# Four mixtures of experts between two attentions: the fourth mixture in tiles of 384 and 256 rows, and three moves in the schedule of the others

## The chip, the core and the metric

One core of one Trainium2 chip. The time is device microseconds of one launch, the median of the runs shown; the profile is one more execution. PE is TensorE, PEld its weight loads, DVE VectorE, ACT ScalarE, POOL GpSimd, SP the queue from which most transfers are issued.

## The reference

4096 tokens of 128 numbers (8 batches of 512), all float32, go through six sublayers, each on a layernorm of x and added to x:

```python
x = x + 0.5 * L0_ffn(layernorm(x))    # mixture 1: 8 experts, top 2, no capacity
x = x + L0_attn(layernorm(x))         # softmax attention, 16 heads, rope
x = x + 0.5 * L0_ffn(layernorm(x))    # mixture 2: same weights
x = x + 0.5 * L1_ffn(layernorm(x))    # mixture 3: 16 experts, top 2, capacity 640
x = x + L1_attn(layernorm(x))         # linear attention
x = x + 0.5 * L1_ffn(layernorm(x))    # mixture 4: weights of mixture 3
# an expert: gelu(rows @ W1 + b1) @ W2 + b2, with W1 128x512 and W2 512x128
# a token whose place among its expert's rows is 640 or more is left out there
```

## The kernel before

Each mixture scatters the normalised rows by expert into a buffer in HBM, reads them back as tiles of 128 rows of one expert, runs the expert, scatters the outputs by token, reads them back by batch and combines them into X. The mixtures are f = 0 to 3 in the code, the sublayers L = 0 to 5 (f = 1 is L 2, f = 2 is L 3, the linear attention is L 4, f = 3 is L 5). There are 71 tiles in f = 0 and 1, and 79 in f = 2 and 3.

A tile takes from PE one transpose (`tile_turn`, L1479), four matmuls of 128 columns into four PSUM banks (`tile_hidden`, L1502) and four more for the output (`tile_outputs`, L1511). ACT makes four gelus (L1091). DVE copies the turned rows (`rows_turned`, L2261), makes the scatter's indices (L2272) and adds the bias (`outputs_out`, L2275). SP loads the tile's 64.5 KB of rows (L642) and its expert's 256 KB of W1 (L645) at addresses read from a table; W2 and the biases of all 16 experts stay in SBUF. POOL scatters the outputs (L846). PE, ACT and DVE look the expert's place up in the table for each tile.

Every engine has its own list of work in a fixed order. The tile loops count steps c: in step c PE turns tile c+2, does `hidden(c)` and then `outputs(c-1)`, and the routing and combining of batches are put into chosen steps. In f = 1, batch b (0 to 7) begins at step `start_of(L, b)`: two gathers (L1985), layernorm moments (L1975) and a root on DVE, scaling on ACT, turning and router logits (L1559) on PE, top two on DVE, ranks (L1413 to L1418) on PE, and slots on DVE (`place`, L2050 to L2060) at `place_of`. POOL then sends the batch's rows to the next mixture in 8 indirect transfers (`send`, L825). The eight starts are 26, 32, 41, 50, 59, 68, 74, 79, and `place_of` is 10 later. The sends of batches 0 to 4 are mixed into f = 1 one for each output scatter, each batch's from the tile after its place.

The tables of tiles are made in two parts. When the first five batches (`KNOWN1`) are counted (`count_first`, L1425), `first_table` (`first_sums`, `first_rows`: a chain of dependent DVE operations, L2160 to L2176) lists the first 25 tiles, which can start before the other batches are routed; `main_counts`, `main_sums` and `main_rows` list the rest. In f = 1 the first sums and rows for f = 2 fall into steps 70 and 71, ahead of the output of tile 70 in DVE's order. The linear attention makes the first table for f = 3 in its iteration 5, while its `logits(5)` waits for it.

f = 2 combines batches 0 to 3 between its tiles (`FRONTS` = 4, at `front_of(b)` = 50, 55, 60, 65), and the linear attention, in iterations 2 to 5, batches 4 to 7. For each of these POOL takes a deviation more there (`deviation_of`, L881 to L885) and ACT two passes instead of one. f = 3 combines six batches between its tiles (`LAST_FRONTS` = 6) and two behind them.

## Time and profile before

| | |
|---|---|
| median of 3 runs | 1451.51 us (1450.81 to 1454.0) |
| the profiled execution, its own time | 1452.39 us |
| its span, first to last instruction | 1450.5 us |
| busy: PE, PEld, DVE, ACT, POOL | 1215.6, 856.8, 916.6, 802.0, 694.4 us |
| mean granted clock of PE | 0.934 |
| moved by DMA | 229.15 MB, mean 158 GB/s |

The stages follow one another: the second mixture's tile loop ends near 903 us, the third's runs to about 1129, the linear attention to 1262, and the fourth mixture to the end. A float32 matmul shows as two records in PE's rows, a transpose as one. "x8" in a row of the timeline is eight such records in a line, and its length is that from the first's start to the last's end.

### The profile page before, as it was taken

To read this page: it belongs to the slowest core of one execution; us is meant where nothing else is said; L and a number is where in the kernel's file an instruction comes from. 1 tells how busy PE (TensorE), PEld (TensorE's weight loads), DVE (VectorE), ACT (ScalarE), POOL (GpSimd) and SP (SyncE) were. 2 spreads that over 40 slices of the span, in tenths; PEclk is the share of its full clock that TensorE was granted. 3 is DMA by queue.
4 is the path that set the end of the run, shared out by engine and by line. 5 is a ranking of instruction groups with operands and counts; after the bars stand their busy time and mean duration, and the time that the engine had idled before them with its cause. 6 is when DMAs were issued, how large, how long until landed. Compare 5 with 4: busy or idle time off the path is not lost.

```text
span 1450.5 us, 34189 instructions
## 1 busy us (share of the span) xinstructions
PE 1215.6 (84%) x8356; PEld 856.8 (59%) x8356; DVE 916.6 (63%) x3275; ACT 802.0 (55%) x2085; POOL 694.4 (48%) x931
## 2 busy tenths in 40 slices
PE   4399897999999998998689897389989766589995
PEld 3399884222323223222589786388978655489995
DVE  7534667889889999886425656363355586543344
ACT  4255542676776776767345554254555564355552
POOL 4776452222253553545644576276434276544443
PEclk9999998899999999999799999599999986599998
DMA  9787767443534524441478684466756021367785
GB/s 292 175 227 209 211 184 223 137 127 114 165 118 127 144 77 132 125 131 36 125 206 255 199 234 122 110 177 183 204 166 183 8 66 38 102 171 197 212 232 173
DMA packets 194060, 229.15 MB, mean 158 GB/s; under 512 B 28304, under 2 KB 129296, under 8 KB 193872
## 3 DMA queue, kind: packets, MB, share of 16 engines
q1 hardware_dynamic: 170704, 187.74, 47.7%
q0 software_dynamic: 17792, 36.60, 7.3%
q10 hardware_dynamic: 5376, 2.63, 0.6%
q8 instruction: 78, 1.28, 0.4%
q14 instruction: 110, 0.90, 0.2%
HBM read 156.85 MB, written 69.76 MB: 156 GB/s over the span
## 4 chain that ended last, share of the span: by engine, by line
PE 55%; DVE 22%; issue 6%; POOL 5%; ACT 5%; DMA 3%; DVEq 2%; SPq 1%; ACTq 0%; POOLq 0%
PE PS L1502 16%; PE PS L1511 15%; DVE arena L2470 6%; PE PS L1693 5%; PE PS L1669 5%; PE PS L1479 3%; POOL dispatched L825 3%; DVE X L1985 2%; ACT arena L1212 2%; PE PS L1677 2%; PE PS L1655 2%; DVE BST L1975 2%; DVEq L2269 1%; DVE arena L2261 1%; DVE arena L2275 1%
## 5 line engine op out<-in xcount | busy, mean ns | idle before, releaser
L1091 ACT ACTIVATE arena<-PS,arena 128x128 f32<-128x128 f32 x1200 | 347.4, 368 | 316.4 <-PE PS L1502 305.6
L846 POOL DMA_INDIRECT expert_out<-arena x300 | 290.8, 969 | 331.3 <-DVE arena L2272 141.3
L1212 ACT ACTIVATE arena<-PS 128x512 f32<-128x512 f32 x512 | 283.8, 596 | 135.4 <-PE PS L1669 134.4
L1502 PE MATMUL PS<-arena 128*128 128x128 f32 x2400 | 343.7, 288 | 8.9 <-ACT arena L1091 7.4
L1511 PE MATMUL PS<-arena 128*128 x2400 | 329.4, 281 | 17.8 <-DVE arena L2275 16.1
L2470 DVE TENSOR_REDUCE arena<-PS 128x2 f32<-128x1024 f32 x256 | 301.0, 1217 | 28.3 <-PE PS L1679 27.4
L1511 PEld LDWEIGHTS PS<-arena 128*128 128x128 f32 x2400 | 299.3, 196 | 24.9 <-issue 22.8
L1502 PEld LDWEIGHTS PS<-arena 128*128 128x128 f32 x2400 | 303.5, 198 | 13.7 <-issue 11.3
L2275 DVE TENSOR_TENSOR arena<-PS,arena 128x128 f32<-128x128 f32 x300 | 87.6, 292 | 232.9 <-PE PS L1511 230.6
L825 POOL DMA_INDIRECT dispatched<-arena x192 | 185.4, 966 | 89.7 <-issue 54.4
L1669 PE MATMUL PS<-arena 96*128 96x512 bf16 x512 | 174.3, 392 | 10.5 <-ACT arena L1212 5.4
L1669 PEld LDWEIGHTS PS<-arena 96*128 96x128 bf16 x512 | 45.0, 98 | 184.2 <-ACT arena L1212 148.7
L1479 PE MATMUL PS<-CST,arena 128*128 128x128 f32 x300 | 90.6, 302 | 73.1 <-DMA arena<-dispatched 36.4
L1693 PE MATMUL PS<-arena 128*18 128x512 f32 x1024 | 136.1, 605 | 1.4 <-ACT arena L1212 0.5
L2272 DVE TENSOR_TENSOR arena<-arena,CST 128x1 uint32<-128x1 f32 x300 | 48.0, 160 | 111.7 <-issue 77.7
L1013 POOL DMA_INDIRECT dispatched<-arena x64 | 62.5, 976 | 108.2 <-DVE arena L2470 92.7
L2261 DVE COPY arena<-PS 128x128 f32<-128x128 f32 x300 | 85.3, 284 | 39.8 <-PE PS L1479 21.8
L1677 PE MATMUL PS<-arena 64*128 64x512 bf16 x256 | 86.2, 398 | 19.5 <-DVE arena L2470 15.0
L1479 PEld LDWEIGHTS PS<-CST,arena 128*128 128x128 f32 x300 | 43.7, 146 | 98.2 <-issue 54.4
L1679 PE MATMUL PS<-arena 64*128 64x512 bf16 x256 | 86.2, 398 | 0.0
L1985 DVE SCALAR_TENSOR_TENSOR X<-YC,GATE,X 128x128 f32<-128x128 f32 x256 | 74.6, 353 | 6.4 <-DMA YC<-expert_out 6.2
L1677 PEld LDWEIGHTS PS<-arena 64*128 64x128 bf16 x256 | 19.0, 94 | 85.8 <-DVE arena L2470 44.4
(264 smaller groups left out, 1196.5 us busy)
## 6 DMA issues: line engine op xcount, KB each, us to landing
arena<-experts SPq DMA_DIRECT2D x300, 256.0 KB
arena<-dispatched SPq DMA_DIRECT2D x300, 64.5 KB
qk_products<-arena SPq DMA_DIRECT2D x48, 384.0 KB, 4.4
arena<-qk_products SPq DMA_DIRECT2D x64, 288.0 KB
YC<-expert_out SPq DMA_DIRECT2D x64, 256.0 KB
dispatched<-FILL SPq DMA_DIRECT2D x32, 322.5 KB, 6.5
arena<-experts SPq DMA_DIRECT2D x32, 322.0 KB, 5.8
arena<-qk_products SPq DMA_DIRECT2D x64, 128.0 KB, 5.2
```

The lines of the kernel that those rows point to most:

```text
L825: pool.indirect_dma_start(buffer_of(L), bass.IndirectOffsetOnAxis(ap=SLOT[:, k, t:t + 1], axis=0), XR[:, k, t, :], None).then_inc(s_first ...
L846: pool.indirect_dma_start(YK, bass.IndirectOffsetOnAxis(ap=ID[:, n:n + 1], axis=0), YS[:, n, :], None).then_inc(s_yo[sign_of(f, tau)], 16)
L1091: act.activation(bent(f, tau)[:, q, :], bank(q, 0, P), func, bias=arena[:, bass.ds(stay + (DOWN + q), 1)]).then_inc(s_g, 1)
L1212: act.activation(PT[:, G % 2, j, k, :], bank(4 + k % 2), ACT.Exp, scale=float(1.0 / np.sqrt(HD))).then_inc(s_exp, 1)
L1479: pe.transpose(bank(4, 0, P), XP[:, g % XRING, 0:D], ident).then_inc(s_xpt, 1)
L1502: pe.matmul(bank(q, 0, P), ups(f, tau)[:, q * P:q * P + P], turned(f, tau), start=True, stop=True).then_inc(s_h, 1)
L1511: mm = pe.matmul(bank(6, 0, P), bent(f, tau)[:, q, :], arena[:, bass.ds(stays[f, tau] + q * D, D)], start=(q == 0), stop=(q == FC - 1))
L1669: pe.matmul(bank(4 + k % 2), KS[0:STACK, G % QK_RING, j, P * k:P * k + P], QS[0:STACK, G % QK_RING, j, :], start=True, stop=True).then_inc ...
L1677: pe.matmul(bank(2 * w), QS[0:HALF, r, head, P * a:P * a + P], KS[0:HALF, r, head, :], start=True, stop=True)
L1693: mm = pe.matmul(bank(6)[32 * j:32 * j + VCOLS, :], VA[:, G // 4 % V_RING * GT + k, q % 2, j, (HD + 1) * o:(HD + 1) * o + VCOLS], PT[:, G ...
L1985: ins = dve.scalar_tensor_tensor(out=X[:, t, :], in0=YC[:, b % 2, k, j, :], scalar=GATE[:, k, t:t + 1], in1=X[:, t, :], op0=ALU.mult, op1= ...
L2470: dve.tensor_reduce(MX[:, G % 2, head:4:2, a], PS[:, 1024 * w:1024 * w + 1024].rearrange("p (a b) -> p a b", a=2), AX_X, ALU.max).then_inc ...
```

## The change

1. The fourth mixture gets functions of its own (`last_sixteen`, `tall_turn`, `tall_hidden`, `tall_gelus`, `tall_outputs`, `tall_rows`, `tall_out`, `late_table`, `tall_moe`). It has 32 tiles: one of the first 384 rows of each expert, and then one of the other 256 rows of each, in the order in which the experts passed 384 rows. A tile loads its whole expert (1156 columns of float32, 592 KB) into a ring of 4 and needs no lookup; the first 16 need no table either. Every matmul of `tall_hidden` has 384 or 256 columns. It starts when all rows have been sent. Nothing of the first table is left in it.
2. The linear attention no longer counts the first five batches nor makes the first table, and `logits(5)` waits for nothing of it.
3. f = 1: the eight starts become 24, 29, 38, 47, 56, 65, 73, 79, and `place_of` is 7 later instead of 10. The outputs of a batch are loaded at `start + 4` in SP's order instead of `start + 2`. `last_step` becomes 90 instead of 93.
4. f = 2: `FRONTS` = 6, at `front_of(b)` = 47, 52, 57, 62, 67, 72, so batches 4 and 5 leave the linear attention. In f = 3 four batches are combined between tiles, and four behind them. ACT issues the loads of the first four.

```diff
-MOE = [dict(E=E0, S=S0, tiles=TOKENS * 2 // (S0 * P) + E0 - 1), dict(E=E1, S=S0, tiles=TOKENS * 2 // (S0 * P) + E1 - 1)]
+MAIN, SHORT = 3, S1 - 3
+MOE = [dict(E=E0, S=S0, tiles=TOKENS * 2 // (S0 * P) + E0 - 1), dict(E=E1, S=S0, tiles=TOKENS * 2 // (S0 * P) + E1 - 1),
+       dict(E=E1, S=MAIN, tiles=2 * E1)]
...
-FRONTS, LAST_FRONTS = 4, 6
+RING = 4
+FRONTS, LAST_FRONTS = 6, 4
...
+        def late_to(b):
+            return E1 + min(E1, (b + 1) * GT * P * 2 // (MAIN * P + 1))
+        def late_front(b):
+            return late_to(b) + 6
...
-            return max(wide_to(b) + 10, 50 + 5 * b)
+            return max(wide_to(b) + 7, 47 + 5 * b)
...
             if carries(L):
                 if b >= NG - 2:
-                    return MOE[0]["tiles"] + 3 + 5 * (b - NG + 2)
-                return max(tiles_to(b) + 8 + b, early_tiles(L) + E0 + 6 + 4 * b)
+                    return MOE[0]["tiles"] + 2 + 6 * (b - NG + 2)
+                return outputs_of(L, b) + 5 + b
...
         def place_of(L, b):
-            return start_of(L, b) + 10
+            return start_of(L, b) + 7
...
+            def last_sixteen(L):
...
+                for tau in range(RING):
+                    expert_in(tau)
+                sp.wait_ge(s_disp, sent_for(L))
+                for tau in range(XRING):
+                    some_rows(tau)
+                for tau in range(RING, tiles):
+                    sp.wait_ge(s_yc, T0 + tau - (RING - 1))
+                    some_rows(tau + XRING - RING)
+                    expert_in(tau)
+                for b in range(LAST_FRONTS, NG):
+                    wait_outputs(sp, f, late_to(b))
+                    load_outputs(sp, L, b)
...
                     pool.nop(nofuse=True)
-                    pool.indirect_dma_start(YK, bass.IndirectOffsetOnAxis(ap=ID[:, n:n + 1], axis=0),
-                                            YS[:, n, :], None).then_inc(s_yo[sign_of(f, tau)], 16)
+                    for n in range(at, at + size(f, tau)):
+                        pool.indirect_dma_start(YK, bass.IndirectOffsetOnAxis(ap=ids[:, n:n + 1], axis=0),
+                                                rows[:, n, :], None).then_inc(s_yo[sign_of(f, tau)], 16)
...
+            def tall_hidden(f, tau):
+                T0, r, N = TILES0[f], tau % RING, size(f, tau) * P
+                pe.wait_ge(s_we[r], 16 * expert_loads(f, tau))
+                pe.wait_ge(s_xpc, T0 + tau + 1)
+                for q in range(FC):
+                    pe.wait_ge(s_g, (T0 + tau - 1) * FC + q + 1)
+                    pe.matmul(bank(q, 0, N), WE[:, r, q * P:q * P + P], XPT3[:, tau % PAIR, 0:N],
+                              start=True, stop=True).then_inc(s_h, 1)
...
+            def tall_moe(L):
+                pe.wait_ge(s_slot, NG * (f + 1))
+                count_all(f, bank(5, 0, NG * E1))
+                tall_turn(f, 0)
+                tall_turn(f, 1)
+                tall_hidden(f, 0)
+                for c in range(1, tiles + 1):
+                    if c + 1 < tiles:
+                        tall_turn(f, c + 1)
+                    if c < tiles:
+                        tall_hidden(f, c)
+                    tall_outputs(f, c - 1)
...
                 def logits(r):
                     pe.wait_ge(s_l2c, r + 1)
-                    if r == KNOWN1:
-                        pe.wait_ge(s_soon, f + 1)
...
-                    if i == KNOWN1:
-                        pe.wait_ge(s_pl, NG + KNOWN1)
-                        count_first(f, bank(4, 256, 256 + KNOWN1 * E1))
...
-                        for b in starting(L, c - 8):
+                        for b in starting(L, c - 6):
                             scores_in(b, E1, bank(5, 0, GT * E1), n + b)
-                        for b in starting(L, c - 9):
+                        for b in starting(L, c - 7):
                             chosen_out(b, E1, n + b)
...
-                    if i == KNOWN1:
-                        first_table(f, bank(4, 256, 256 + KNOWN1 * E))
```

## Rows read from the trace of the kernel before

**Rows 1.** The page, part 4: the chain that ended last, by engine.
```profile
PE 55%; DVE 22%; issue 6%; POOL 5%; ACT 5%; DMA 3%; DVEq 2%; SPq 1%; ACTq 0%; POOLq 0%
```

**Rows 2.** Windows: length; busy (instructions) of PE, PEld, DVE, ACT, POOL; clock, DMA, GB/s.
```profile
715.00:903.00 188.00, 163.81 (x1281) 154.61 (x1281) 97.67 (x515) 94.90 (x313) 105.64 (x110) 0.95 0.70 202
903.00:926.00 23.00, 0.66 (x4) 0.42 (x4) 6.90 (x38) 2.77 (x6) 8.67 (x10) 0.57 0.18 55
1129.00:1262.00 133.00, 88.47 (x460) 73.24 (x458) 90.58 (x446) 71.09 (x175) 74.48 (x107) 0.75 0.18 52
1279.00:1436.00 157.00, 151.44 (x1247) 144.54 (x1247) 64.44 (x286) 83.83 (x292) 71.38 (x74) 1.00 0.73 200
```

**Rows 3.** Timeline (start, length, engine, line, [idle before <-releaser]), second mixture to third.
```profile
901.59 1.15 PE L1511 MATMUL PS<-arena 128*128 x8 [0.68 <-DVE arena L2275]
...
903.63 0.23 DVE L2116 TENSOR_SCALAR arena<-PS 128x80 f32<-128x80 f32 x1
...
909.94 0.29 DVE L2275 TENSOR_TENSOR arena<-PS,arena 128x128 f32<-128x128 f32 x1
...
921.07 0.96 POOL L825 DMA_INDIRECT dispatched<-arena  x1 [0.30 <-issue]
924.56 0.36 SPq L642 DMA_DIRECT2D arena<-dispatched  x1
...
926.34 0.48 PE L1479 MATMUL PS<-CST,arena 128*128 128x128 f32 x1 [20.27 <-DMA arena<-dispatched]
```

**Rows 4.** Timeline of PE around the third mixture's batch 2.
```profile
1085.56 0.30 PE L1479 MATMUL PS<-CST,arena 128*128 128x128 f32 x1
...
1095.93 0.30 PE L1479 MATMUL PS<-CST,arena 128*128 128x128 f32 x1
```

**Rows 5.** Timeline of DVE in the linear attention: residuals (L2652), first table.
```profile
1168.05 0.69 DVE L2652 TENSOR_TENSOR X<-PS,X 128x512 f32<-128x512 f32 x1 [0.51 <-PE PS L1904]
...
1181.91 0.69 DVE L2652 TENSOR_TENSOR X<-PS,X 128x512 f32<-128x512 f32 x1 [0.50 <-PE PS L1904]
...
1213.09 0.69 DVE L2652 TENSOR_TENSOR X<-PS,X 128x512 f32<-128x512 f32 x1 [0.94 <-PE PS L1904]
...
1221.37 0.07 DVE L2160 MEMSET arena<- 128x16 f32 x1 [4.95 <-PE PS L1425]
...
1226.89 0.29 DVE L2634 TENSOR_TENSOR arena<-PS,CST 128x128 f32<-128x128 f32 x1
```

**Rows 6.** Timeline of POOL there: a deviation and the send behind it.
```profile
1163.94 1.05 POOL L881 TENSOR_TENSOR LN<-LN 128x4 f32<-128x4 f32 x1
...
1166.63 1.09 POOL L825 DMA_INDIRECT dispatched<-arena  x1 [0.52 <-issue]
```

**Rows 7.** Timeline at the start of the fourth mixture.
```profile
1260.97 0.17 DVE L2060 CAST arena<-arena 128x8 uint32<-128x8 f32 x1
...
1262.05 0.45 PE L1479 MATMUL PS<-CST,arena 128*128 128x128 f32 x1 [2.02 <-DVE arena L2060]
...
1264.13 2.05 PE L1502 MATMUL PS<-arena 128*128 128x128 f32 x8
...
1271.21 0.96 POOL L825 DMA_INDIRECT dispatched<-arena  x1 [0.30 <-issue]
```

**Rows 8.** Timeline: two rounds of the tile loop; and four matmuls of 256 columns.
```profile
1422.74 0.97 PEld L1511 LDWEIGHTS PS<-arena 128*128 128x128 f32 x8
...
1424.63 0.97 PEld L1511 LDWEIGHTS PS<-arena 128*128 128x128 f32 x8
...
1133.47 1.89 PE L1867 MATMUL PS<-WT,XT 128*128 128x256 f32 x8
```

**Rows 9.** Chain of waits, last 16 us (start, length, what).
```profile
1435.08 1.17 PE PS L1511 x8
...
1437.41 3.58 DMA expert_out<-arena
...
1441.57 3.40 DMA YC<-expert_out
```

More of the change, by code:

```diff
@@ L394, in moe_of, with tall @@
         def moe_of(f):
-            return MOE[0 if FFNS[f] == FFN0 else 1]
+            return MOE[(0, 0, 1, 2)[f]]
+        def tall(f):
+            return moe_of(f)["S"] > 1
         def first_kind(f):
@@ L407, in expert_loads, with size @@
         def expert_loads(f, tau):
+            if tall(f):
+                return len(range(tau % RING, TILES0[f], UPS)) + tau // RING + 1
             return on_all(f, tau) // UPS + 1
+        def size(f, tau):
+            return SHORT if tall(f) and tau >= E1 else moe_of(f)["S"]
         def turned(f, tau):
@@ L448, in scattered, with out_ring, shared_by @@
         def scattered(f, r, n):
-            return sum(16 for tau in range(n) if sign_of(f, tau) == r)
-        def sign_of(f, tau):
-            return tau % BLOCKS // PAIR
+            return sum(16 * size(f, tau) for tau in range(n) if sign_of(f, tau) == r)
+        def out_ring(f):
+            return BLOCKS // moe_of(f)["S"]
+        def shared_by(f):
+            return 1 if tall(f) else PAIR
+        def sign_of(f, tau):
+            return tau % out_ring(f) // shared_by(f)
+        def late_to(b):
+            return E1 + min(E1, (b + 1) * GT * P * 2 // (MAIN * P + 1))
+        def late_front(b):
+            return late_to(b) + 6
         def wide_to(b):
@@ L802, in _ @@
                     eight(L)
+                elif kind == FFN1 and not tall(ffn_of(L)):
+                    sixteen(L)
                 elif kind == FFN1:
-                    sixteen(L)
+                    last_sixteen(L)
                 elif kind == ATTN:
@@ L841, in scatter @@
                 def scatter(tau):
-                    n = tau % BLOCKS
+                    at = tau % out_ring(f) * m["S"]
+                    ids, rows = (ID3, YS3) if tall(f) else (ID, YS)
                     pool.wait_ge(s_id, T0 + tau + 1)
@@ L1162, in moe @@
                         gap_exp(f + 1)
-                    if L == len(SUBLAYERS) - 1 and c == 2:
-                        gap_exp(f)
+                    for b in range(LAST_FRONTS):
+                        if tall(f) and late_front(b) == c + 3:
+                            wait_outputs(act, f, late_to(b))
+                            load_outputs(act, L, b)
                     for b in range(2):
@@ L2291, in even_gates, with kept_gates @@
                     chain(dve.tensor_scalar(GATE[:, k, :], gates[k], 0.5, None, ALU.mult))
+            def kept_gates(f):
+                r = [R1[:, k, :] for k in range(20)]
+                gates = shares(f)
+                for k in range(2):
+                    chain(dve.scalar_tensor_tensor(out=r[14], in0=PICK[:, k, :], scalar=-float(REGION),
+                                                   in1=r[9 + k], op0=ALU.mult, op1=ALU.add))
+                    chain(dve.tensor_scalar(r[11 + k], r[14], float(CAPACITY), None, ALU.is_lt))
+                    chain(dve.tensor_tensor(r[17 + k], gates[k], r[11 + k], ALU.mult))
+                chain(dve.tensor_tensor(r[13], r[17], r[18], ALU.add))
+                chain(dve.tensor_scalar(r[14], r[13], 1e-9, None, ALU.add))
+                chain(dve.reciprocal(r[15], r[14]))
+                for k in range(2):
+                    chain(dve.scalar_tensor_tensor(out=GATE[:, k, :], in0=r[17 + k], scalar=0.5, in1=r[15],
+                                                   op0=ALU.mult, op1=ALU.mult))
@@ new lines, in tall_moe @@
+            def tall_moe(L):
+                f = ffn_of(L)
+                tiles = moe_of(f)["tiles"]
+                score_gap(f)
+                kept_gates(f)
+                tall_rows(f, 0)
+                tall_rows(f, 1)
+                for c in range(1, tiles + 1):
+                    if c + 1 < tiles:
+                        tall_rows(f, c + 1)
+                    for b in range(LAST_FRONTS):
+                        if late_front(b) == c:
+                            gather(f, b, 0)
+                    tall_out(f, c - 1)
+                    if c == 3:
+                        late_table(f)
+                    for b in range(LAST_FRONTS):
+                        if late_front(b) == c:
+                            gather(f, b, 1)
+                for b in range(LAST_FRONTS, NG):
+                    gather(f, b, 0)
+                    gather(f, b, 1)
@@ L2362, in moe @@
                         even_gates(f)
-                    if handed(L) and c == begin(L) + 4 or L == len(SUBLAYERS) - 1 and c == 8:
-                        kept_gates()
+                    if handed(L) and c == begin(L) + 4:
+                        kept_gates(f)
                     for b in fronts:
@@ L2450, in moe @@
                             main_rows(f + 1)
-                if L == len(SUBLAYERS) - 1:
-                    for b in range(LAST_FRONTS, NG):
-                        gather(f, b, 0)
-                        gather(f, b, 1)
             def attention(L):
@@ L2714, in _ @@
             for L, kind in enumerate(SUBLAYERS):
-                if kind in (FFN0, FFN1):
+                if kind == FFN1 and tall(ffn_of(L)):
+                    tall_moe(L)
+                elif kind in (FFN0, FFN1):
                     moe(L)
```

170 lines of the change are left out of this document (122 added, 48 removed).

## The prediction

> **What bounds the kernel now.** I read the chain of waits first, then the windows by stage, then the timeline at each seam. Over half of the chain is PE and a fifth DVE [rows 1], but the windows tell the stages apart [rows 2]. In the tile loops PE is the limit: 151.44 us busy of 157 in the fourth mixture, and 163.81 of 188 in the second, where routing is mixed in. From 903 to 926 nobody does anything of weight: PE is busy 0.66 us of 23. In the linear attention PE is busy 88 us of 133 and DVE 91, so there a chain through all engines sets the pace. The change touches one loop, one hole and that chain. I cost it in that order of time, against the profiled execution's 1452.39 us; the median of the runs is 0.88 lower.
>
> **Second mixture to third.** The last tile's matmuls end at 902.74, but its copy comes at 909.94, since the first table's 5.5 us (903.63 to 909.1) stand ahead of it on DVE. POOL, in order, waits with that tile's scatter. Then come 8 sends at 1.26 each (0.96 and 0.30 idle), the last at 921.07. SP issues the first row load at 924.56, and PE turns the first tile at 926.34 [rows 3]. In the new order batch 4 is placed at step 63, so its sends go out one with each of tiles 64 to 70: seven are gone when the last tile is scattered, and one is left. From the copy to the last send it took 11.13 us; seven sends fewer make 2.3. Then 3.49 to the row load and 1.78 to the turn, as in the rows, and 0.6 for a batch's 512 KB that now stand right ahead in SP's queue: the first turn comes 8.2 us after the copy. The copy no longer waits for the table, so it would be at 903.1. But the table now lies at steps 64 and 65 inside the loop, where a step has little room on DVE, and batch 5's turning, logits and scores come before tile 70 too. I take 5 us for both; the bounds are 2 (half of the table hidden, since DVE is busy only 98 of 188 us there) and 8 (nothing hidden). So the first turn is at 903.1 + 5 + 8.2 = 916.3, 10.0 earlier. Behind it DVE has a gather and a batch's moments less to do before tile 1, at least 2 us of it on PE's path as both wait for the same rows: **-12.0** in all.
>
> The rest of the closer routing steps I cost at nothing, bounds -2 and +3: the same instructions run, the ranks now wait for DVE within their own step (some 0.5 us for each of 6 batches), and the slots no longer fall on the step of the next batch's moments. The outputs are loaded 3 steps ahead of their gather instead of 5, some 7 us. That covers 4.2 us from a scatter's start to a load's start (1437.41 to 1441.57) [rows 9] only for batches whose last tile is a few steps old, and batch 0 is the tight one, 1 us at most.
>
> **Two more batches within the third mixture.** Around batch 2, four tiles take 10.37 us [rows 4]. Four take 7.6 at the floor of 1.89 [rows 8] and 8.6 at the fourth mixture's mean (1247 records in 157 us, 17 a tile, 2.14). So a batch costs 1.8 to 2.8; I take 2.2, for two **+4.4**.
>
> **Linear attention, the table.** DVE sat idle 4.95 us for the count, which PE makes only behind batch 7's projections, and worked from 1221.37 to 1226.89 on the table; only then came the masking (L2634) on which PE's next numerators wait [rows 5]. Without the table DVE masks during the projections, and PE goes straight on where the count was. That is 5.5 us and the 0.7 of count, masking and their waits: **-6.2**, bounds -4 and -8, since DVE or ACT may be next in line in the same iteration. What is late next is ACT's scaling of the batch.
>
> **Linear attention, POOL.** A deviation takes 2.69 us from its start to the next send, 2.53 more than the gap it fills [rows 6]. An iteration with 8 sends and 2 deviations is 10.1 + 5.1 = 15.2 us of POOL. The iterations take 13.86 us while POOL is not yet behind, and the next two 31.18 together [rows 5]. Batches 4 and 5 lose one deviation each, so POOL is 5.1 less behind, and these two iterations can fall towards 2 x 13.9: **-3.4**, bounds 0 and -5. Both batches' gathers leave DVE there too, which is in the bound.
>
> **Fourth mixture, start.** Before, PE turned the first tile 1.1 us after the last slots, its rows being long there. The last send started at 1271.21 [rows 7]. Now everything waits for it: 3.49 to the row load, then 1.78 for 64.5 KB [rows 3]. For three times the rows I take 2.5 (bounds 1.8 and 4). That is 1277.2, so **15.2 later**. The four first experts are loaded well before. The gates' chain on DVE and the table load on ACT, which lay between tiles before, fall into this wait.
>
> **Fourth mixture, loop.** A tile of 17 records costs 1.89 us at best, 0.111 each; eight records of 256 columns take 1.89 with the last one's drain (0.17 more than its columns), so 0.213 each [rows 8]. The cost follows the columns, and 384 make 0.320. A tall tile is then 3 x 0.111 + 8 x 0.320 + 24 x 0.111 = 5.56, a short one 0.22 + 1.71 + 1.78 = 3.70, all 32 together 148.2 us. 79 old ones at 1.89 would be 149.1: the wider matmuls save almost nothing by themselves. What they save is the room between 1.89 and 2.14, since each wait and lookup now comes once in 2 or 3 blocks. Before, it took from 1262.05 to 1436.23 [rows 7, 9], 174.2 us. Now: 2.7 from the rows to the first wide matmul (two turns of three and a copy), 148.2 less 0.7 for these turns, 1.5 for gaps (bounds 0 and 6), 0.7 before the last outputs, and 2 for the half clock (1.2 in place of 2.4 GHz) at which a start after a wait runs (the first eight records took 2.05 us, half of it would be 1.03 [rows 7]). That is 154.4, **-19.8**. DVE's copies become at most 0.69 (128x512 [rows 5]) in a step of 3.7 or more, ACT has half as many gelus of more columns and was busy 84 of 157 us [rows 2], POOL needs 2 or 3 x 1.26. None comes near.
>
> **Fourth mixture, transfers.** A short tile moves 592 + 132 + 128 = 852 KB in 3.70 us, 230 GB/s, and 2.1 MB of batches beside 16 of them. The old loop moved 200 GB/s at a share of 0.73 [rows 2]. By that ratio 274 would be full. I take **+1.5**, bounds 0 and 20.
>
> **Fourth mixture, end.** The last scatter started at 1437.41, its batch was there 7.66 us later [rows 9], and two gathers and the store took the rest to 1450.5. Now the last tile has two scatters (+1.4). Behind them batches 6 and 7 both wait, and 7's load starts only when batch 5, itself gathered at about 9.5 us past PE's end, is done with the buffer. Loads of 3.6 us, gathers of 2.3 and a store of 3.1 put the end 18.6 us after PE's, against 14.3: **+4.4**, bounds +2 and +7.
>
> **The sum.** -12.0 + 4.4 - 6.2 - 3.4 + 15.2 - 19.8 + 1.5 + 4.4 = -15.9, so 1436.5 on the profiled execution and 1435.6 as a median.
>
> **The rivals.**
> (a) The hole between second and third mixture stays, because POOL is behind: scatter and send are 2.53 us a tile against 2.6 to 2.7 of the loop, and now begin five tiles earlier. Then only -12 is lost: 1447.6. Against it: before, POOL had idle gaps on DVE at that load. 10%.
> (b) The linear attention gives only 4 of its 9.6, another engine being next: 1441. 15%.
> (c) More is gained: the table hides in the loop, the start's half clock is short, the hole shrinks by 17 or more: 1427. 12%.
> (d) The other side: the wide experts outrun the DMA. If 200 GB/s were the ceiling, a short tile would take 4.26 and the batches 10.5 more: +18 on the forecast, 1453.8, no change. Below that it decides: at 180 GB/s, 4.73 a tile and 11.7, +27, 1462. For it: 230 exceeds anything the old loop held. Against it: the share of 0.73. 4% for over 1454.4.
> (e) Wide records cost less than their columns. If one of 384 cost no more than 0.111, 26.7 + 13.0 us would go: 1396. Rows 8 speak against it, as 256 columns took 0.213. 2%. The Trainium skill ("TensorE: Matmul & The Clock Gate", section "Back-to-back issue gap") gives a sustained 81 ns a matmul at 128 columns and 131 at 512, by which wide ones would be much cheaper for each column; the trace does not agree.
>
> **How the numbers follow.** The forecast, 1429 to 1442, has 57%, and the five above 43. 1422 to 1448 takes in (a) to (c) and leaves out (d), (e) and some tails. A measurement can tell 0.2%, 2.9 us: within 1448.6 to 1454.4 I see the upper part of (a) and the lower of (d), 5%; slower 4%; faster 91%.
>
> **What would show it.** Right: PE's first turn of the third mixture some 8 us after the last copy of the second; linear iterations of about 14 us and no 22 us one; the fourth's first turn about 15 us after the last slots; 5.6 and 3.7 us a tile; 18 to 19 us behind PE's end. Wrong: PE waiting for an expert load in the short tiles, or POOL's scatter of tile 70 many microseconds behind its copy.

## The result, and the profile of the changed kernel

| | before | after |
|---|---|---|
| median of 7 runs | 1452.05 us (1449.92 to 1457.27) | 1458.80 us (1456.89 to 1463.15) |
| profiled execution, its span | 1452.39, 1450.5 | 1459.03, 1457.2 |
| PE's granted clock, mean | 0.934 | 0.935 |

The ratio of after to before is 1.0045, with a 95% interval of 1.0026 to 1.0064. The change makes the kernel slower, where 1435.6 us and a gain of 1.1% was forecast. A repaired version among the experiments below, e9, takes 1442.6 us, 0.9931 of before (0.9909 to 0.9953).

Six landmarks that both kernels have, read from timelines of DVE, cut the span into stages: the copy of a tile's outputs (`outputs_out`, before L2275, after L2413) for tiles 22, 63 and 70 of the second mixture and for the first tile of the third, and the cast that ends a batch's slots (L2060, after L2198) for batches 0 and 7 of the linear attention. All times in us; the last column is the forecast for the stage.

| stage | before | after | difference | forecast |
|---|---|---|---|---|
| start to tile 22 | 773.5 | 772.5 | -1.0 | 0 |
| tile 22 to tile 63 | 110.8 | 126.9 | +16.1 | 0 (-2 to +3) |
| tile 63 to tile 70 | 25.7 | 25.1 | -0.6 | } |
| tile 70 to the third mixture's first copy | 29.4 | 24.4 | -5.0 | } -12.0 for both |
| third mixture to batch 0's slots | 217.7 | 224.9 | +7.2 | +4.4 |
| linear attention, slots 0 to slots 7 | 103.9 | 93.0 | -10.9 | -9.6 |
| fourth mixture, slots 7 to the end | 189.5 | 190.4 | +0.9 | +1.3 |

The last row's forecast is 15.2 - 19.8 + 1.5 + 4.4. Of the 22.6 us between the forecast (-15.9) and the spans' difference (+6.7), 16.1 are in one stage that I had costed at nothing, 6.4 behind it up to the third mixture's first copy, and 2.8 in the third mixture; the first row and the last two give 2.7 back. A stage time is that of one profiled execution, and executions of one kernel differ by several us in all, so differences of 1 or 2 us between stages carry nothing by themselves.

In windows of the changed kernel (length; busy time and instructions of PE, PEld, DVE, ACT, POOL; clock, DMA share, GB/s) the stages correspond to those of before [rows 2]:

```profile
714.00:922.00 208.00, 170.27 (x1285) 160.66 (x1285) 102.72 (x545) 98.70 (x319) 108.73 (x114) 0.93 0.65 184
925.00:936.00 11.00, 0.78 (x6) 0.38 (x6) 5.43 (x26) 0.00 (x0) 8.26 (x10) 0.55 0.42 119
1146.00:1267.00 121.00, 82.24 (x467) 68.32 (x466) 78.76 (x384) 70.95 (x169) 70.23 (x98) 0.82 0.17 56
1284.00:1438.00 154.00, 151.32 (x973) 129.20 (x972) 40.48 (x132) 65.58 (x128) 73.70 (x77) 0.99 0.61 189
```

The first line is the second mixture's loop: PE executes nearly the same number of matmuls as in the first of [rows 2], but needs 208 us for them in place of 188, and 38 of them are idle, against 24. The second line is the hole behind it, 11 us in place of 23.

What ended PE's idle time in the loop stands in the waits from 740 to 925 us (engine, tile and line that waited, who released it: us in all, times, the longest). Before:

```profile
PE PS L1479 <- DVE arena L2261: 10.2, 10, 1.4
...
PE PS L1511 <- DVE arena L2275: 7.4, 7, 1.3
```

After, with DVE's own new wait:

```profile
PE PS L1613 <- DVE arena L2413: 14.8, 6, 4.0
...
DVE X L2123 <- DMA YC<-expert_out: 10.9, 5, 3.6
PE PS L1581 <- DVE arena L2399: 9.5, 9, 1.6
...
PE PS L1515 <- DVE arena L2177: 7.2, 5, 3.4
```

Two waits are new. DVE's gather (L2123) waits for the load of the batch's expert outputs into YC at each of batches 0 to 4 (3.1, 0.9, 3.6, 2.7 and 0.5 us); before, no such wait is listed. The copy of the tile's outputs is queued behind the gather on DVE, and PE's next outputs (L1613) wait for that copy. And PE's ranks (L1515) wait for the choices that DVE makes in the same step. One such place, from the timeline of the changed kernel at batch 0:

```profile
772.30 0.94 SPq L619 DMA_DIRECT2D YC<-expert_out  x2
...
776.08 1.14 DVE L2123 SCALAR_TENSOR_TENSOR X<-YC,GATE,X 128x128 f32<-128x128 f32 x4 [3.08 <-DMA YC<-expert_out]
...
778.04 0.29 DVE L2413 TENSOR_TENSOR arena<-PS,arena 128x128 f32<-128x128 f32 x1
...
778.57 1.48 PE L1613 MATMUL PS<-arena 128*128 x8 [3.09 <-DVE arena L2413]
...
780.12 1.94 PE L1604 MATMUL PS<-arena 128*128 128x128 f32 x8
```

DVE stands 3.08 us, PE 3.09, and PE pays once more: the eight records that follow take 1.94 us, where the same eight took 1.12 before the stall. Windows of these two stretches, the stall and what follows (columns as above):

```profile
775.00:778.50 3.50, 0.48 (x5) 0.29 (x3) 1.75 (x8) 1.09 (x4) 0.00 (x0) 1.00 0.81 231
778.50:782.00 3.50, 3.43 (x18) 3.35 (x19) 2.76 (x16) 0.98 (x3) 1.64 (x2) 0.61 0.69 222
```

The granted clock is 1.00 while PE is idle for most of 3.5 us, and 0.61 in the 3.5 us in which it works again: partly the lower of its two levels (1.2 in place of 2.4 GHz). The same follows the stall at batch 2 (PE idle until 825.61), with a clock of 0.65 from 826 to 829.5.

### The profile page after: what moved, and what is told of

It reads as the page before. It is cut to its first block, busy times and chain, and to the rows that moved or that the text cites. A ratio compares the mean times of both kernels' runs of the same rounds, so it can differ in the third digit from the quotient of the medians.

```text
span 1457.2 us, 30877 instructions
## 1 busy us (share of the span) xinstructions
PE 1200.4 (82%) x7988; PEld 830.5 (57%) x7988; DVE 893.2 (61%) x3114; ACT 775.0 (53%) x1888; POOL 690.4 (47%) x922
## 4 chain that ended last, share of the span: by engine, by line
PE 49%; DVE 20%; DMA 9%; issue 6%; ACT 5%; POOL 5%; SPq 3%; DVEq 1%; ACTq 0%; POOLq 0%
PE PS L1604 9%; PE PS L1613 9%; DVE arena L2657 6%; PE PS L1834 5%; PE PS L1810 5%; PE PS L1640 4%; PE PS L1631 4%; POOL dispatched L909 3%; DMA YC<-expert_out 3%; DVE X L2123 3%; ACT arena L1314 2%; PE PS L1581 2%; PE PS L1818 2%; PE PS L1796 2%; DVE BST L2113 1%
## 5 line engine op out<-in xcount | busy, mean ns | idle before, releaser
L1177 ACT ACTIVATE arena<-PS,arena 128x128 f32<-128x128 f32 x884 | 257.5, 369 | 264.2 <-PE PS L1604 255.3
L2657 DVE TENSOR_REDUCE arena<-PS 128x2 f32<-128x1024 f32 x256 | 300.9, 1216 | 26.2 <-PE PS L1820 25.3
L1613 PE MATMUL PS<-arena 128*128 x1768 | 248.9, 285 | 23.7 <-DVE arena L2413 21.6
L1604 PE MATMUL PS<-arena 128*128 128x128 f32 x1768 | 257.8, 292 | 7.8 <-ACT arena L1177 7.2
L1613 PEld LDWEIGHTS PS<-arena 128*128 128x128 f32 x1768 | 226.7, 200 | 28.9 <-issue 28.0
L1604 PEld LDWEIGHTS PS<-arena 128*128 128x128 f32 x1768 | 228.9, 202 | 10.3 <-issue 9.5
L2413 DVE TENSOR_TENSOR arena<-PS,arena 128x128 f32<-128x128 f32 x221 | 64.5, 292 | 167.6 <-PE PS L1613 166.4
L1186 ACT ACTIVATE arena<-PS,arena 128x384 f32<-128x384 f32 (+1 forms) x128 | 65.6, 529 | 100.0 <-PE PS L1631 97.1
L1581 PE MATMUL PS<-CST,arena 128*128 128x128 f32 x221 | 67.6, 306 | 58.8 <-DMA arena<-dispatched 27.9
L2123 DVE SCALAR_TENSOR_TENSOR X<-YC,GATE,X 128x128 f32<-128x128 f32 x256 | 74.8, 354 | 20.1 <-DMA YC<-expert_out 19.8
L2410 DVE TENSOR_TENSOR arena<-arena,CST 128x1 uint32<-128x1 f32 x221 | 35.2, 159 | 83.7 <-issue 54.4
L2463 DVE TENSOR_TENSOR arena<-PS,arena 128x384 f32<-128x384 f32 (+1 forms) x32 | 15.7, 492 | 108.5 <-PE PS L1640 108.5
L2399 DVE COPY arena<-PS 128x128 f32<-128x128 f32 x221 | 63.0, 285 | 28.5 <-PE PS L1581 21.5
```

The lines of the kernel that those rows point to most:

```text
L1177: act.activation(bent(f, tau)[:, q, :], bank(q, 0, P), func, bias=arena[:, bass.ds(stay + (DOWN + q), 1)]).then_inc(s_g, 1)
L1581: pe.transpose(bank(4, 0, P), XP[:, g % XRING, 0:D], ident).then_inc(s_xpt, 1)
L1604: pe.matmul(bank(q, 0, P), ups(f, tau)[:, q * P:q * P + P], turned(f, tau), start=True, stop=True).then_inc(s_h, 1)
L1613: mm = pe.matmul(bank(6, 0, P), bent(f, tau)[:, q, :], arena[:, bass.ds(stays[f, tau] + q * D, D)], start=(q == 0), stop=(q == FC - 1))
L2123: ins = dve.scalar_tensor_tensor(out=X[:, t, :], in0=YC[:, b % 2, k, j, :], scalar=GATE[:, k, t:t + 1], in1=X[:, t, :], op0=ALU.mult, op1= ...
L2657: dve.tensor_reduce(MX[:, G % 2, head:4:2, a], PS[:, 1024 * w:1024 * w + 1024].rearrange("p (a b) -> p a b", a=2), AX_X, ALU.max).then_inc ...
```

## Why the load comes late

SP loads the rows of tile g when the copy of tile g - 8 is done (`rows_in` waits for `s_yc`), and the batch load hangs on SP's own tile number. At start + 2, as before, it stands behind the copy of tile start - 6; at start + 4 behind that of start - 4. The gather itself follows the copy of tile start - 2. Batch 2 before (its start is 41), SP's and DVE's timelines:

```profile
808.14 0.29 DVE L2275 TENSOR_TENSOR arena<-PS,arena 128x128 f32<-128x128 f32 x1 [1.37 <-PE PS L1511]
...
810.99 0.93 SPq L579 DMA_DIRECT2D YC<-expert_out  x2
...
818.18 1.13 DVE L1985 SCALAR_TENSOR_TENSOR X<-YC,GATE,X 128x128 f32<-128x128 f32 x4
```

And after (its start is 38):

```profile
813.96 0.29 DVE L2413 TENSOR_TENSOR arena<-PS,arena 128x128 f32<-128x128 f32 x1
...
814.42 0.33 SPq L682 DMA_DIRECT2D arena<-dispatched  x1
814.99 1.09 SPq L685 DMA_DIRECT2D arena<-experts  x1
816.12 0.44 SPq L674 DMA_DIRECT2D arena<-experts  x1
816.94 0.93 SPq L619 DMA_DIRECT2D YC<-expert_out  x2
...
823.11 1.14 DVE L2123 SCALAR_TENSOR_TENSOR X<-YC,GATE,X 128x128 f32<-128x128 f32 x4 [3.58 <-DMA YC<-expert_out]
```

Before, the load is issued 7.2 us ahead of its gather. After, the gather was due at 819.53 (823.11 less its wait), 2.6 us behind the load, since three issues of SP's stand between the copy and the load. The load took 3.8 us at batch 0 (772.30 to 776.08) and 6.2 at batch 2.

Batch 0 has a second cause on top. There SP had come to its load at 770.1, and stood until 772.2 for the scatters of the batch's last tiles to land (SP's waits from 768 to 775 us):

```profile
SPq L624 <- DMA expert_out<-arena: 1.9, 1, 1.9
```

At batches 1 to 4 it did not stand there at all. So at batch 0 the start itself, two steps earlier than before, is too near to the scatters, and at the others only SP's order makes the load late. For comparison, the Trainium skill ("DMA: Bandwidth & Descriptors", section "Anatomy of one DMA — SWDGE (gpsimd) path") gives about 2.0 us and the bytes at 436 GB/s for a single DMA of another path; for 512 KB I estimate 3.2 from it, which only batch 0 comes near. That the rest comes from the row and expert loads that run beside it is argued and not measured.

This was theory A1. The rivals: A3, that the closer steps (ranks in their choices' step, batches 0 and 1 five steps apart) are the cost; A2, that an earlier load would wait for its last scatter anyway (which batch 0 shows in part); and B, that the loop is slower for something outside this part.

## The experiments

All ratios are to the kernel before, run on the same chip beside them, with 95% intervals. The stages of each, in us, as in the first table:

| kernel | 22 to 63 | 63 to 70 | to third | third | linear | fourth | span |
|---|---|---|---|---|---|---|---|
| before | 110.8 | 25.7 | 29.4 | 217.7 | 103.9 | 189.5 | 1450.5 |
| after | 126.9 | 25.1 | 24.4 | 224.9 | 93.0 | 190.4 | 1457.2 |
| e1 | 111.1 | 25.6 | 29.0 | 224.6 | 93.2 | 189.0 | 1445.6 |
| e2 | 115.4 | 25.7 | 22.7 | 227.7 | 93.0 | 187.6 | 1447.7 |
| e3 | 112.1 | 24.9 | 25.8 | 226.8 | 94.1 | 188.8 | 1446.9 |
| e4 | 127.2 | 25.0 | 24.3 | 218.0 | 96.4 | 188.4 | 1456.3 |
| e5 | 126.4 | 25.2 | 21.9 | 217.2 | 100.4 | 189.8 | 1456.2 |
| e6 | 114.0 | 25.3 | 22.9 | 228.3 | 92.9 | 189.3 | 1447.5 |
| e7 | 129.9 | 25.7 | 29.1 | 219.7 | 100.5 | 193.3 | 1472.2 |
| e8 | 116.0 | 25.4 | 23.5 | 227.8 | 92.9 | 188.6 | 1447.8 |
| e9 | 114.0 | 25.4 | 25.3 | 221.5 | 93.0 | 187.9 | 1441.0 |
| e10 | 114.9 | 25.4 | 23.6 | 221.6 | 93.0 | 189.1 | 1446.9 |
| e11 | 114.9 | 25.4 | 22.7 | 224.3 | 93.0 | 187.9 | 1443.6 |
| e12 | 113.9 | 25.4 | 23.3 | 217.0 | 104.0 | 190.2 | 1450.7 |

Tile 22's copy falls between 772.5 and 777.1 in all but e10, where it is at 779.3. The stages are those of each run's profiled execution, which is not always near its median: e1's took 1447.4 us with a median of 1452.6, e7's 1474.0 with 1469.8, and e12's 1452.5 with 1448.6.

**e1: the second mixture as before, the rest changed.** From the changed kernel:

```
-                    return MOE[0]["tiles"] + 2 + 6 * (b - NG + 2)
-                return outputs_of(L, b) + 5 + b
+                    return MOE[0]["tiles"] + 3 + 5 * (b - NG + 2)
+                return max(tiles_to(b) + 8 + b, early_tiles(L) + E0 + 6 + 4 * b)
...
-            return start_of(L, b) + 7
+            return start_of(L, b) + 10
```

with the load at start + 2 and every offset (4, 6, 6, 8, 8, 9, 10) as before.

> The changed kernel with the second mixture's combining and routing at the steps of before (starts, loads, offsets, ranks 10 steps behind the gather); all else is of the change. Theory A (the closer steps cost 15.15 us in the loop up to tile 63 and give back 5.5 from there to the first copy of the third mixture): the copy of tile 63 comes near 884 again, the handover takes some 29 us from the last copy, and the time is 1458.8 - 15.15 + 5.5 = 1449, 1446 to 1451. Rival B (the loop is slower for a reason outside these steps, such as the transfers or the place of the code): 1457 to 1460.

Measured: 1452.64 us median, ratio 0.9996 (0.9980 to 1.0013). The loop from tile 22 to 63 is back at 111.1 and the handover at 29.0, both as before. The median is above my range of 1446 to 1451, while the profiled execution, with 1447.38, lies within it; its runs lay between 1445.5 and 1453.8 at clocks from 0.941 to 0.931. The loop's loss is in the second mixture's steps, so rival B falls. And all other parts of the change together, with the third mixture's late loads among them (e4, e9), bring nothing that can be measured.

**e5: the reverse, this part alone on the kernel before.**

> The kernel before with this one part of the change alone: the second mixture's starts, loads and close steps are the new ones. Theory A: +15.15 in the loop and -5.5 at the handover, so about 10 us slower than before, 1459 to 1464. Rival B (the loss needs the other parts): 1447 to 1453. What I forecast for this part was -12.

Measured: 1459.39 us, ratio 1.0052 (1.0033 to 1.0072), about 7.5 us slower than before; I had expected about 10 and named 1459 to 1464. The loop takes 126.4. The part that I had forecast at -12 costs by itself about what the whole change costs.

**e2: only the load's step undone.**

```
-                        if start_of(L, b) + (4 if carries(L) else 2) == tau:
+                        if start_of(L, b) + 2 == tau:
```

> The changed kernel, but SP issues the load of a batch's outputs at start + 2 of its own count, as before, in place of start + 4, so 2 tiles (some 5.2 us) earlier. Theory A1 (the load is what comes late: DVE's gathers waited 10.9 us for it in five waits, PE waited 7.4 us more than before for DVE's copies): 1458.8 - 8 = 1451, 1448 to 1453, and the gather's waits for the load are gone. Rival A2 (the load would wait for the last scatter anyway, SP then stands in its wait instead): 1457 to 1460, with SP's waits for the scattered outputs longer. Rival A3 (PE's waits for ranks and the nearness of two batches are the cost): 1455 to 1458.

Measured: 1449.21 us, ratio 0.9983 (0.9966 to 1.0001), so one number in SP's order is worth some 9 us (1.0045 less 0.9983 of 1452). The loop falls by 11.5 to 115.4. The waits of e2 from 740 to 920 us:

```profile
PE PS L1515 <- DVE arena L2177: 9.2, 6, 3.4
...
PE PS L1613 <- DVE arena L2413: 5.4, 3, 4.0
...
DVE X L2123 <- DMA YC<-expert_out: 1.0, 1, 1.0
```

DVE's wait for loads fell from 10.9 to 1.0, PE's for DVE's copies from 14.8 to 5.4. A1 holds. A2 falls but for batch 0: SP stands there from 769.5 to 773.0 for the scatters, and the 1.0 us that is left of DVE's wait is that batch's. The waits for ranks stayed, as A3 would have them, but cost far less.

**e7: only the load's step changed, on the kernel before.**

```
-                        if start_of(L, b) + 2 == tau:
+                        if min(start_of(L, b) + (4 if carries(L) else 2), tiles - 1) == tau:
```

> The kernel before, all its steps kept, with the load of batches 0 to 4 of the second mixture issued 2 tiles later (start + 4, batch 5 at the last tile). Theory A1 (two tiles later the load lands behind its gather, whatever the steps): DVE waits 8 to 11 us for it in five waits and the loop is 5 to 9 us longer, 1456 to 1461. Rival (only the earlier starts made the load late, so here it is still in time): 1450 to 1453.

Measured: 1469.79 us, ratio 1.0112 (1.0091 to 1.0132): 16 to 18 us, about twice what I gave it. Its waits from 740 to 930 us:

```profile
PE PS L1511 <- DVE arena L2275: 15.9, 9, 4.1
...
DVE X L1985 <- DMA YC<-expert_out: 14.7, 5, 4.1
```

No close step, no earlier start, and yet the same waits, even longer. The loop's +19.1 is more than the 14.7 of DVE's waits. In the window from tile 22 to tile 63, before and in e7,

```profile
773.46:884.27 110.81, 95.84 (x768) 90.34 (x768) 66.71 (x360) 58.96 (x192) 63.58 (x67) 0.97 0.74 217
774.05:903.95 129.90, 104.47 (x768) 99.53 (x767) 67.25 (x360) 59.94 (x192) 63.24 (x66) 0.88 0.64 184
```

PE is idle for 10.5 us more, and for the other 8.6 it is busy longer with the same 768 records, at a granted clock of 0.88 in place of 0.97. A load two tiles late is enough for a loss of this size by itself. In the changed kernel, undoing it gave back 11.5 of the loop's 16.1 (e2); the other 4.6 are with the closer steps and the earlier starts (e3).

**e3: starts and loads as before, the close steps kept.**

> The changed kernel with the starts and the loads of before (batches begin at steps 26, 32, 41, 50, 59, 68, 74, 79 less or more), but with the new close steps: turn 4, logits 5, ranks and slots 7 behind the gather. Batch 4 is placed at step 66, so four of its eight sends lie inside the loop. Theory A1 (late loads): all of the loop's loss but the ranks' waits (some 3 to 4 us) goes, and half of the handover's gain stays: 1446, 1443 to 1450. Rival A3 (the close steps themselves cost, since ranks and scores wait within their step): the loop keeps 8 us or more of its loss, 1452 to 1456.

Measured: 1450.72 us, ratio 0.9992 (0.9978 to 1.0006), just above A1's range and below A3's. The loop takes 112.1, so the close steps by themselves cost 1.3 us there, although PE waits 7.1 us in five for the ranks here too. The 3.3 us more of e2 are with the earlier starts, of which batches 0 and 1 stand five steps apart and not six.

**e6: loads at start + 2, and ranks and slots a step later.**

```
-                    return MOE[0]["tiles"] + 2 + 6 * (b - NG + 2)
+                    return MOE[0]["tiles"] + 2 + 5 * (b - NG + 2)
...
-            return start_of(L, b) + 7
+            return start_of(L, b) + 8
...
-                        if start_of(L, b) + (4 if carries(L) else 2) == tau:
+                        if start_of(L, b) + 2 == tau:
...
-                        for b in starting(L, c - 7):
+                        for b in starting(L, c - 8):
                             carried_ranks(b)
```

> The changed kernel with the loads at start + 2 and with ranks and slots 8 steps behind the gather in place of 7 (the last batch starts one step earlier, so that the mixture ends at the same step). With the load alone moved, PE waited 9.2 us in six waits for the choices that DVE makes in the ranks' own step, longest 3.4. Theory A (these waits are on the path): 9 us less in the loop before, 1449.2 - 5 to - 8, so 1441 to 1445. Rival B (PE would stand in its turns or in DVE's copies instead, DVE being late by the same work): 1448 to 1450, with the waits under another name.

Measured: 1447.71 us, ratio 0.9964 (0.9947 to 0.9981). That is 1.5 us below e2 by the medians and 2.8 by the ratios, within the two intervals, and not 5 to 8. PE's waits for ranks fell from 9.2 us in six to 1.9 in one, but those for DVE's copies are 8.5 in place of 5.4, and 2.5 us for ACT's gelus are new:

```profile
PE PS L1613 <- DVE arena L2413: 8.5, 6, 4.0
...
PE PS L1613 <- ACT arena L1177: 2.5, 6, 0.8
...
PE PS L1515 <- DVE arena L2177: 1.9, 1, 1.9
```

Rival B had it nearly right: when PE waits for an engine that is itself late, taking the wait away at one place moves it to the next.

**e8: e6, and batch 1 a step later.**

> As the kernel with the ranks a step later, with batch 1 one step later as well (start 30 in place of 29), so that its gather and moments fall further from batch 0's scores and choices. Theory A (batches 0 and 1, five steps apart, cost 8.6 us more than in the kernel before up to tile 31, partly by the ranks' wait of 3.4, partly by DVE's crowding): 1 to 3 us below that kernel. Rival B (the crowding was the wait only): the same within 1 us.

Measured: 1448.70 us, ratio 0.9976 (0.9965 to 0.9986), so nothing gained against e6; tile 31 comes 27.4 us after tile 22 in place of 28.7, and later tiles give that back. Both are above before's 21.2. What of that stretch belongs to the crowding of two batches and what to the work that is done earlier stays open.

**e4: four batches in the third mixture, as before.**

```
-FRONTS, LAST_FRONTS = 6, 4
+FRONTS, LAST_FRONTS = 4, 4
...
-            return max(wide_to(b) + 7, 47 + 5 * b)
+            return max(wide_to(b) + 10, 50 + 5 * b)
...
-                        if front_of(b) + 4 == tau:
+                        if front_of(b) + 2 == tau:
```

> The changed kernel with the third mixture combining four batches between its tiles, at the steps and with the loads of before, so that the linear attention combines four itself; the first table stays out of the linear attention. My forecast priced the two batches at +4.4 in the third mixture and -3.4 in the linear attention, so undoing them gives 1458.8 - 1.0 = 1457.8. Theory A (the third mixture is 7.1 us longer for them): third mixture near 218 us again from its first copy to the linear attention's first slots, the linear attention 3 to 5 longer, 1454 to 1457. Rival B (the 7.1 come from running the mixture straight after a stalled handover): third mixture stays at 223 or more, 1460 to 1463.

Measured: 1455.11 us, ratio 1.0017 (1.0002 to 1.0031), so about 4 below after: theory A. The third mixture takes 218.0 (-6.9) and the linear attention 96.4 (+3.4). The relief of POOL is what I had put it at, 3.4; the two batches cost 7 and not 4.4. But the run also puts this mixture's loads back by two tiles, so the 7 are for both. Where the surplus sits is seen in e6's DVE timeline at the third mixture's batch 0:

```profile
1046.07 1.14 DVE L2123 SCALAR_TENSOR_TENSOR X<-YC,GATE,X 128x128 f32<-128x128 f32 x4 [3.46 <-DMA YC<-expert_out]
```

Its load had been issued at 1040.12. The change moved this loop's loads from front + 2 to front + 4 as well, which neither its description nor the forecast mentions. It is the same fault a second time; in the changed kernel itself the gather waited 2.28 us there.

**e9: e6, with the third mixture's loads at front + 2 too.**

> The kernel with the second mixture's loads 2 tiles earlier and its ranks a step later, and now the third mixture's loads 2 tiles earlier too (front + 2 in place of front + 4). There, at batch 0, DVE waited 3.46 us for the load, and five tiles took 19.2 us where the kernel before took 11.1. Theory A (late loads are the common cause): that stretch falls to 13 to 15 us, the third mixture from its first copy to the linear attention's first slots from 228.3 to 222 to 225, and the time from 1447.7 to 1442 to 1445. Rival B (the stretch is long because batch 0's gather, moments and the linear attention's first turn crowd into it): still over 17 us, and 1447 to 1449.

Measured: 1442.60 us (1441.63 to 1443.08), ratio 0.9931 (0.9909 to 0.9953). This beats both kernels: 9.8 us below before, 5 below e6. The stretch of five tiles (the copies of tiles 45 to 50) takes 14.0 us in place of e6's 19.2, the third mixture 221.5. DVE's first gather there starts at 1045.88 with no wait:

```profile
1045.88 1.16 DVE L2123 SCALAR_TENSOR_TENSOR X<-YC,GATE,X 128x128 f32<-128x128 f32 x4
```

With loads in time, the two more batches cost 3.8 us by this stage (221.5 against 217.7). Against e12, whose second mixture is e9's, it is 4.5, and 6.5 with the stage ahead of it.

**e10: the loads another 2 tiles earlier.**

> As the kernel with both loads 2 tiles earlier, but 4 tiles earlier than in the changed kernel (at start and at front). Theory A says that the wait for the last scatter then bounds the load, SP standing in it with eight row loads ahead: within 1.5 us of that kernel either way, DVE's waits for loads under 1 us. Rival C (SP's wait for the scatter holds back the row and expert loads behind it): PE waits for rows, 2 to 8 us slower.

Measured: 1448.57 us, ratio 0.9978 (0.9965 to 0.9992), 6 us slower than e9: rival C. It is worst at batch 0. SP:

```profile
763.55 0.43 SPq L674 DMA_DIRECT2D arena<-experts  x1
771.54 0.95 SPq L619 DMA_DIRECT2D YC<-expert_out  x2
773.59 0.35 SPq L682 DMA_DIRECT2D arena<-dispatched  x1
```

and PE:

```profile
776.12 0.33 PE L1581 MATMUL PS<-CST,arena 128*128 128x128 f32 x1 [4.11 <-DMA arena<-dispatched]
```

SP stands 7.5 us in its waits for the scatters of tiles that aren't made or landed yet, the row loads stand behind it, and PE runs out of rows. At batch 1 the same costs PE 2.05 us (at 790.68); at batches 2 and 3 SP stands 4 to 5 us, but the rows last. So the load has a window: at start + 4 it is too late, at start too early for batches 0 and 1. The Trainium skill ("DMA: Bandwidth & Descriptors", section "Anatomy of one DMA — SWDGE (gpsimd) path") says that a semaphore wait for a DMA is made by the issuing sequencer and not by the DMA engines; these rows agree.

**e11: e9 with the third mixture's batches a step later.**

> As the kernel with both loads 2 tiles earlier, with the third mixture's six batches a step later each (48 + 5 b in place of 47 + 5 b). If a load is still a little late for batch 0, 1 to 3 us below that kernel; if not, the same within 1 us, or 1 us more as the linear attention's own first batch starts later.

Measured: 1441.90 us, ratio 0.9929 (0.9905 to 0.9952), the same as e9 within the noise. A step more or less for the batches there makes no difference.

**e12: the repaired part alone, on the kernel before.**

> The kernel before with the second mixture's new starts alone, its loads at start + 2 and its ranks 8 steps behind the gather. It says what the closer steps are worth once nothing waits for a load. My forecast for them was -12. Theory A, by the times from the copy of tile 22 to the third mixture's first copy (165.9 before, 162.2 in the changed kernel so mended): 3.7 us faster than before, 1446 to 1449.5; the ranks and the crowding of the batches then eat the rest of the 12. Rival (the 12 were there but for the loads): 1438 to 1442.

Measured: 1448.56 us, ratio 0.9970 (0.9950 to 0.9990), 4 us faster than before, with an interval of 1.5 to 7. So the closer steps are worth about 4 us once hardly anything waits for a load, not 12.

## Why the prediction was wrong, step by step

**The closer routing steps, "at nothing, bounds -2 and +3".** This is the step that failed. The loop lost 16.1 us. The sentence "the outputs are loaded 3 steps ahead of their gather instead of 5, some 7 us" took the lead too long: I counted steps from SP's tile number without what SP's row load waits for. The copies between the one that frees SP and the gather were four before and two after, of which SP's own three issues take another 3 us: 7.2 us before, 2.6 after. Against this lead I held the 4.2 us from a scatter's start to a load's start [rows 9], so the need for scatters to land, and priced nothing for the load itself: 3.40 us in the same rows, and 3.8 to 6.2 within the loop. I named only batch 0 as tight, for 1 us at most, where batches 0 to 4 all waited. Batch 0 is tight for the reason I gave, the scatters (SP stood 1.9 us there), but the others are not. e2, e5 and e7 show that the load's place is the cause of most of the loss. My own sign for a wrong forecast had looked at PE's expert loads and POOL's scatter, and at neither the gather nor YC.

**"The ranks now wait for DVE, 0.5 us for each."** They waited 7.2 us in five waits, longest 3.4. But most of that is time by which DVE is late in any case: e3 has 7.1 us of them in a loop only 1.3 longer than before, and e6, which takes most of them away, won 1.5.

**Second mixture to third, -12.** Measured -5.6 from tile 63's copy on. Three terms were mis-sized, and none alone. From tile 63 to 70 I had 23.9 (25.7, less the 6.8 by which tile 70's copy was to come earlier, plus 5 for table and batch 5); it takes 25.1. The first turn came 10.9 us after tile 70's copy in place of 8.2. And the 2 us that DVE was to spare before the third mixture's first copy did not come: from first turn to first copy it takes 13.5 us (935.47 to 948.98), before 13.0; in e2 and e5, with the same steps there, it is 11.9 and 11.1. Together 6.4, the difference to -12.

The 10.9 begins with a miscount. POOL's timeline behind tile 70's copy (924.56), after:

```profile
925.73 0.96 POOL L932 DMA_INDIRECT expert_out<-arena  x1 [0.30 <-issue]
927.00 0.96 POOL L909 DMA_INDIRECT dispatched<-arena  x1 [0.30 <-issue]
928.26 0.96 POOL L909 DMA_INDIRECT dispatched<-arena  x1 [0.30 <-issue]
```

A send stands behind each scatter in POOL's order, so the send of tile 70's step comes after tile 70's scatter, and two early sends are left there, not one. The last starts at 928.26, 3.7 us after the copy in place of 2.3. Rival (a), that POOL is behind, doesn't hold: the scatter starts 1.17 us after its copy, before 1.04. From the last send SP's first row load follows 5.07 us later (933.33), and not 3.49 as in [rows 3]. The chain of waits there, after:

```profile
927.00 0.33 POOL dispatched L909
927.32 0.93 issue
928.26 3.95 DMA dispatched<-arena
```

The send's landing took 3.95 us; in the kernel before the same piece of the chain is

```profile
921.07 2.36 DMA dispatched<-arena
```

Behind this send POOL now goes straight on with batch 5's sends, and SP issues batch 7's outputs (512 KB) at 928.26. The runs sort by this: the time from the last early send to the first row load is 3.4 to 3.5 us in before, e1, e3 and e7, where neither stands behind the send; 5.0 to 5.2 in after, e2, e4 and e5, where both start with it or right behind it; and 4.2 to 4.8 in e6 and e8 to e12, where the outputs' load starts some 0.9 us ahead of it. That these slow the landing fits; the two always come together, so which of them does it stays open. The 0.6 us that I had for the outputs' place in SP's queue passes while SP waits for the send.

**Third mixture, +4.4.** Measured +7.2, of which e9 gives back 3.4 once the loads are in time. The term itself was about right (3.8 by this stage, 4.5 to 6.5 against e12), and the transfer that was moved with it was overlooked.

**Linear attention, table -6.2 and POOL -3.4.** Measured -10.9. The split is in e4: 3.4 for POOL, and 4.0 to 7.5 for the table, since the stage without the change took 100.4 (e5), 100.5 (e7), 104.0 (e12) and 103.9 (before). After, the slots follow each other by 13.8, 13.7, 13.8, 13.6, 15.7 us; the 22.2 of before is gone.

**Fourth mixture.** The stage took +0.9 where the terms make +1.3. The last send starts at 1277.08, the rows are issued at 1279.38, and PE begins at 1282.05, 15.2 after the last slots. Before, it was 1.1 after them, so this is 14.1 later and not the 15.2 of the term: the rows follow the send by 2.30 us, the send's landing, where I had taken 3.49 from a place at which SP still read the first tile's address behind the landing. PE's lines:

```profile
1282.05 0.91 PE L1622 MATMUL PS<-CST,arena 128*128 128x128 f32 x3 [14.69 <-DMA arena<-dispatched]
...
1284.43 4.43 PE L1631 MATMUL PS<-arena 128*128 128x384 f32 x8
1288.70 0.49 PE L1622 MATMUL PS<-CST,arena 128*128 128x128 f32 x3
1289.03 2.75 PE L1631 MATMUL PS<-arena 128*128 128x384 f32 x8
1291.61 2.84 PE L1640 MATMUL PS<-arena 128*128 128x128 f32 x24
1294.29 0.49 PE L1622 MATMUL PS<-CST,arena 128*128 128x128 f32 x3
```

From PE's first turn to its end the loop takes 156.2 us (154.4 and 1.5 for transfers forecast). From turn to turn a tall tile takes 5.59 us (forecast 5.56), a short one 3.73 (3.70). Eight records of 384 columns take 2.75 with the last one's drain, so 0.322 each: cost follows columns. Rival (e) falls, and with it the rate of the Trainium skill ("TensorE: Matmul & The Clock Gate", section "Back-to-back issue gap") as a price for these float32 records. The first eight took 4.43, at a granted clock of 0.52 in the window from 1284 to 1288. DMA moved 189 GB/s on average over the loop and PE waited 2.0 us for an expert once, so rival (d) falls. Rival (b) falls with the linear attention's 10.9. PE ended at 1438.2 and the span 19.0 later (18.6 forecast):

```profile
1438.02 2.23 DMA expert_out<-arena
...
1440.68 4.20 DMA YC<-expert_out
...
1447.78 4.27 DMA YC<-expert_out
```

**What is left of the gain.** With both loads in time (e9) the stages sum to +0.5 - 1.2 + 3.8 - 10.9 - 1.6 = -9.4, which is the spans' difference (1441.0 against 1450.5). The forecast of -15.9 was then too good mainly in the second mixture, by 11: of the 4.4 us that the closer steps win behind tile 63, the loop before it takes back 3.2.

## What to carry to other kernels

When a schedule is drawn together, list for each consumer the event that releases its transfer, not the number that the code gives it: the distance from that event, less what the issuing queue does first, must cover the longest landing seen in the loop. And what the transfer itself waits for (here the scatters) must have landed by then. Look in the changed trace for a new pair "engine <- DMA" first; here a shift by two tiles, with nothing else changed, cost 16 us by itself. And a transfer issued from a queue that also feeds the loop can't simply be moved far ahead, since its wait holds up the feed.

## What the runs showed of the hardware that I had not expected

A load of the same 512 KB took from 3.8 to 6.2 us from issue to the gather's start within one loop. A stall of 3 us on PE was followed by eight matmul records in 1.94 us that took 1.12 before it, with a granted clock of 0.61 in that stretch; so e7's loop grew by 19.1 us, where DVE waited 14.7: of the 19.1, 10.5 are idle time of PE and 8.6 longer records. And a send's landing took 3.95 us where it took 2.36 and 2.28 (at 921.07 before, at 1277.08 after) with nothing queued behind it.
